# First layer's gate projection moved to its output stage, and a three-tile projection in the second input stage

## What is computed

```python
# layer 0, state-space part, 8 frames (images) to a sequence, 4 sequences
xz = einsum('bld,ed->ble', layer_norm(x_flat, ln1_w, ln1_b), in_proj_w)   # 96 -> 384
xm, z = split(xz, 2)                                                      # 192 and 192
y_f = ssm_branch(xm, z, ...)            # ... return y * silu(z)
y_b = ssm_branch(reversed xm and z, ...)[reversed]
x_m = x_flat + einsum('ble,de->bld', y_f + y_b, out_proj_w)               # then ln2
# layer 1
x = x + conv_ref(group_norm(x), W_in, b_in, ...)   # W_in: 96 -> 384, halves xx and z of 192
```

## Time and profile before

| what | value |
|---|---|
| median of 3 executions | 18361.85 us (18345.74 to 18377.84) |
| profiled execution, its own time | 18362.69 us |
| its span, first to last instruction | 18360.9 us |
| TensorE, VectorE, ScalarE, GpSimd busy in the whole span | 88%, 87%, 79%, 61% |
| mean granted TensorE clock | 0.962 of full |
| the input stage of layer 0 | from 0 to about 359 us |
| the output stage of layer 0 | from about 5499 to 5969 us |
| the input stage of layer 1 | from about 7216 to 7700 us |

### The profile page before, as it was taken

How to read it: one execution, slowest core, us unless ns; L and a number is a source line. 1 busy time by engine, 2 the same in 40 slices (tenths; PEclk the granted TensorE clock), 3 DMA queues, 4 the chain that set the end, 5 groups by cost and what they waited for, 6 DMA issues and landing times. The chain is left out here.

```text
span 18360.9 us, 268147 instructions
## 1 busy us (share of the span) xinstructions
PE 16077.0 (88%) x94216; PEld 11444.0 (62%) x94216; DVE 15910.4 (87%) x12063; ACT 14529.2 (79%) x23238; POOL 11254.5 (61%) x6343
## 2 busy tenths in 40 slices
PE   8799998899996788879888888888888888889798
PEld 3355554455552365455688888888888888647374
DVE  4799998799996486479899999999999999879698
ACT  7699996799992555557899999999999999745556
POOL 0099993499990475035688888888888888500201
PEclk9899999899997899989999999999999999999899
DMA  5788886788879677767777777777777777741323
GB/s 178 231 243 250 246 252 208 233 249 247 251 223 245 213 226 217 265 230 278 224 191 200 194 192 191 194 193 192 191 190 197 197 191 191 194 122 55 104 57 101
DMA packets 1043305, 3693.66 MB, mean 201 GB/s; under 512 B 162006, under 2 KB 196410, under 8 KB 1017404
## 3 DMA queue, kind: packets, MB, share of 16 engines
q1 hardware_dynamic: 815420, 3003.46, 53.8%
q0 software_dynamic: 147456, 536.94, 14.9%
q10 hardware_dynamic: 79104, 136.10, 2.4%
HBM read 2342.15 MB, written 796.94 MB: 171 GB/s over the span
## 5 line engine op out<-in xcount | busy, mean ns | idle before, releaser
L1832 DVE TENSOR_TENSOR_SCAN l1s_h<-l1s_da,l1s_pd 128x1024 f32<-128x1024 f32 x3072 | 6709.3, 2262 | 152.0 <-DMA l1s_h<-l1s_h 85.4
L1853 ACT ACTIVATE l1s_da<-l1s_dl,l1s_a 128x1024 f32<-128x1024 f32 x3072 | 3505.0, 1141 | 312.7 <-DVE l1s_h L1832 308.5
L1718 PE MATMUL l1s_pd<-l1s_bd,l1s_dut 128*128 128x128 f32 x18432 | 2847.5, 291 | 853.7 <-DVE l1s_h L1832 828.6
L1718 PEld LDWEIGHTS l1s_pd<-l1s_bd,l1s_dut 128*128 128x128 f32 x18432 | 2297.3, 191 | 1229.0 <-DVE l1s_h L1832 1092.0
L1870 ACT ACTIVATE l1s_dm<-l1s_dut,l1s_bt 128x384 f32<-128x384 f32 x5120 | 2888.2, 602 | 200.9 <-PE l1s_pd L1723 200.5
L1687 POOL TENSOR_TENSOR l1s_pb<-l1s_h,l1s_cc 128x1024 f32<-128x1024 f32 x1024 | 2423.4, 2367 | 843.7 <-DVE l1s_h L1832 802.6
L1687 POOL TENSOR_TENSOR l1s_pa<-l1s_h,l1s_cc 128x1024 f32<-128x1024 f32 x1024 | 2428.0, 2371 | 84.1 <-DMA l1s_h<-l1s_h 84.1
L1723 PE MATMUL l1s_pd<-l1s_id,l1s_dm 128*128 128x128 f32 x15360 | 2186.6, 273 | 0.1
L2702 POOL TENSOR_TENSOR l0sf_pr<-l0sf_h,l0sf_cc 128x1024 f32<-128x1024 f32 x768 | 1810.9, 2375 | 32.2 <-DVE l0sf_h L2784 27.0
L2702 POOL TENSOR_TENSOR l0sb_pr<-l0sb_h,l0sb_cc 128x1024 f32<-128x1024 f32 x768 | 1809.1, 2371 | 30.8 <-DVE l0sb_h L2784 26.8
L1723 PEld LDWEIGHTS l1s_pd<-l1s_id,l1s_dm 128*128 128x128 f32 x15360 | 1789.4, 142 | 0.6 <-ACT l1s_dm L1870 0.5
(11 more groups left out here) (323 smaller groups left out, 31362.7 us busy)
## 6 DMA issues: line engine op xcount, KB each, us to landing
l1s_cc<-crows SPq DMA_DIRECT2D x1024, 512.0 KB, 4.5
l1s_h<-l1s_h POOLq DMA_DIRECT2D x1024, 512.0 KB, 6.9
l0sf_cc<-l0crowsf SPq DMA_DIRECT2D x512, 512.0 KB, 6.3
l0sb_cc<-l0crowsb SPq DMA_DIRECT2D x512, 512.0 KB, 5.7
l0sf_cc<-l0crowsf SPq DMA_DIRECT2D x512, 256.0 KB, 8.5
l0sb_cc<-l0crowsb SPq DMA_DIRECT2D x512, 256.0 KB, 7.6
dls<-l1p_dl SPq DMA_DIRECT2D x192, 512.0 KB, 7.0
duts<-l1p_dut SPq DMA_DIRECT2D x64, 1536.0 KB, 6.6
```

The costliest lines, as they stand in the source:

```text
L1718: pe.matmul(pd[:, s % 2, blk * 128:blk * 128 + 128], dut[:, half, blk, j * 128:j * 128 + 128], bd[:, n, blk - SCALED, :], start=True, stop ...
L1832: dve.tensor_tensor_scan(tile(rnd, j), da[:, j, :], pd[:, s % 2, :], 0.0, ALU.mult, ALU.add)\
L1853: act.activation(da[:, j, :], dl[:, half, j, :], ACT.Exp, scale=a[:, HT * half + j, n:n + 1])\
```

## The change

The input stage of layer 0 no longer projects z. It projects the 192 outputs of xm as 128 + 64 rows, TensorE in the order var (k+1), mean (k+2), tiles of image k; ScalarE copies the first tile out, VectorE the second; the table of Ln and Exp is loaded once; and the normalised input is stored to DRAM (`xns`, 96 rows an image) in place of silu(z) (192 rows). The output stage loads those 96 rows as `zin`, projects z itself three images ahead (`widen`, as two tiles), and ScalarE applies Silu out of PSUM (`gate_of`), with tables loaded by name ahead of each. The output projection's PSUM tile is now single. The second layer's input stage has three tiles of 128 outputs; the middle one is emptied half by VectorE and half by ScalarE with Silu, the slot alternates by image, and the tables are loaded early, two to an image.

```diff
 def l0_in_proj(nc, x, w, xmp, xns):
-        out = r.sb("out", [C, 2, 4, HW])
+        out = r.sb("out", [128, 2, 2, HW])
@@ sync
-                        for q in range(4):
-                            sp.wait_ge(evac, nth(4 * k + q))
+                        sp.wait_ge(xnd, nth(k))
+                        sp.sem_inc(passed, 1)
+                        sp.dma_start(one(xns, FRAMES * s + c), xn[:, s, :]).then_inc(s_xn[s], 16)
+                        for q, (done, rows) in enumerate(((evac, slice(0, DLOW)), (evacd, slice(DLOW, DI)))):
+                            sp.wait_ge(done, nth(k))
                             sp.sem_inc(passed, 1)
-                            rows = slice((q % 2) * C, (q % 2 + 1) * C)
...
+                            sp.dma_start(xmp[s, rows, bass.ds(c * HW + PAD, HW)], out[0:rows.stop - rows.start, s % 2, q, :])\
+                              .then_inc(s_out[s % 2][q], 16)
@@ tensor
                 def project(k, s, q):
-                    pe.wait_ge(evac, nth(4 * k + q - 2))
+                    rows = DLOW if q == 0 else DHIGH
+                    pe.wait_ge(evac if q == 0 else evacd, nth(k - 1))
                     for hs in HALVES:
-                        mm = pe.matmul(pp[:, q % 2, hs], wt[:, q * C:(q + 1) * C], xn[:, s % 2, hs], start=True, stop=True)
+                        mm = pe.matmul(pp[0:rows, q, hs], wt[:, q * DLOW:q * DLOW + rows], xn[:, s, hs], start=True, stop=True)
                 def turn(c, s):
                     k = c * SEQS + s
-                    if there(k):
-                        pe.wait_ge(xnd, nth(k))
-                        for q in range(2):
-                            project(k, s, q)
                     c1, s1, k1 = ahead(c, s, 1)
                     if there(k1):
                         pe.wait_ge(sqr, nth(k1))
                         average(k1, s1 % 2, sq[:, s1 % 2, :]).then_inc(var, 1)
-                    if there(k):
-                        for q in range(2, 4):
-                            project(k, s, q)
                     c2, s2, k2 = ahead(c, s, 2)
                     if there(k2):
                         pe.wait_ge(s_in[s2], c2 * 16 + 16)
                         pe.wait_ge(lnv, nth(k2 - 2))
                         average(k2, s2 % 2, xin[:, s2, :]).then_inc(mean, 1)
+                    if there(k):
+                        pe.wait_ge(xnd, nth(k))
+                        project(k, s, 0)
+                        project(k, s, 1)
@@ vector: cent of k+2 first, then xn of k+1, then
+                    if there(k):
+                        dve.wait_ge(proj, nth(2 * k + 1))
+                        dve.wait_ge(s_out[s % 2][1], (k - s % 2) * 8)
+                        dve.tensor_copy(out[0:DHIGH, s % 2, 1, :], pp[0:DHIGH, 1, :]).then_inc(evacd, 1)
@@ scalar: the table's load moved ahead of the turns; Ln, Exp, Square, then
+                    if there(k):
+                        act.wait_ge(proj, nth(2 * k))
+                        act.wait_ge(s_out[s % 2][0], (k - s % 2) * 8)
+                        act.activation(out[:, s % 2, 0, :], pp[:, 0, :], ACT.Copy).then_inc(evac, 1)

 def l0_out_proj(nc, x, ysf, ysb, xns, w, xm, n2):
-        po = r.ps("po", [C, 2, HW]); pm = r.ps("pm", [C, 2, HW])
+        po = r.ps("po", [C, HW]); pm = r.ps("pm", [C, 2, HW]); pz = r.ps("pz", [128, HW])
@@ sync, load
+                    sp.dma_start(zin[:, s, :], one(xns, FRAMES * s + c)).then_inc(s_zin[s], 16)
...
-                    sp.dma_start(z[:, s, 0, :], one(zs[:, 0:DLOW, :], image)).then_inc(s_in[s], 16)
-                    sp.dma_start(z[0:DHIGH, s, 1, :], one(zs[:, DLOW:DI, :], image)).then_inc(s_in[s], 16)
                     sp.dma_start(xin[:, s, :], one(x, image)).then_inc(s_in[s], 16)
@@ tensor
+                def widen(k, s, q):
+                    rows = DLOW if q == 0 else DHIGH
+                    pe.wait_ge(silu, nth(2 * k + q - 1))
+                    for hs in HALVES:
+                        mm = pe.matmul(pz[0:rows, hs], wz[:, q * DLOW:q * DLOW + rows], zin[:, s, hs], start=True, stop=True)
+                    mm.then_inc(wide, 1)
...
+                    if there(k3):
+                        pe.wait_ge(s_zin[s3], c3 * 16 + 16)
+                        widen(k3, s3, 0)
                     if there(k):
                         pe.wait_ge(sqr, nth(k))
                         average(s % 2, sq).then_inc(var, 1)
...
                         average(s1 % 2, xo).then_inc(mean, 1)
+                    if there(k3):
+                        widen(k3, s3, 1)
                     if there(k2):
                         pe.wait_ge(gate, nth(2 * k2 + 1))
-                        pe.wait_ge(resid, nth(k2 - 2))
+                        pe.wait_ge(resid, nth(k2 - 1))
@@ scalar
-                act.preload_act_table_set("natural_log_exp_and_others")
+                def gate_of(k, s, q):
+                    rows = slice(0, DLOW if q == 0 else DHIGH)
+                    act.wait_ge(wide, nth(2 * k + q))
+                    act.wait_ge(proj, nth(k - SEQS))
+                    act.activation(z[rows, s, q, :], pz[rows, :], ACT.Silu).then_inc(silu, 1)
...
+                    if there(k3):
+                        act.preload_act_table(ACT.Silu)
+                        gate_of(k3, s3, 0)
+                    act.preload_act_table_set("natural_log_exp_and_others")
                     if there(k):
... Ln and Exp of image k
+                    if there(k3):
+                        act.preload_act_table(ACT.Silu)
+                        gate_of(k3, s3, 1)
                     if there(k1):
... Square of image k+1

 def l1_in_proj
-        out = r.sb("out", [128, 4, HW])
+        out = r.sb("out", [128, 3, HW])
@@ vector
-                        for q in (0, 1):
-                            dve.wait_ge(proj, nth(4 * k + q))
+                        for q, rows in ((0, slice(0, 128)), (1, slice(0, DHIGH))):
+                            dve.wait_ge(proj, nth(3 * k + q))
                             dve.wait_ge(s_out[q], k * 16)
-                            dve.tensor_scalar(out[:, q, :], pp[:, q % 2, :], bi[:, q:q + 1], None, ALU.add).then_inc(evacd, 1)
+                            dve.tensor_scalar(out[rows, q, :], pp[rows, (s + q) % 2, :], bi[rows, q:q + 1], None, ALU.add)\
+                               .then_inc(evacd, 1)
@@ tensor
-                        pe.wait_ge(evac, nth(2 * (k - 1) + q % 2))
-                        if q >= 2:
-                            pe.wait_ge(evacd, nth(2 * k + q % 2))
+                        if q < 2:
+                            pe.wait_ge(evac, nth(2 * (k - 1) + q))
+                        if q == 0:
+                            pe.wait_ge(evacd, nth(2 * (k - 1) + 1))
+                        if q == 2:
+                            pe.wait_ge(evacd, nth(2 * k))
                         for hs in HALVES:
-                            mm = pe.matmul(pp[0:m, q % 2, hs], wi[:, at:at + m], xc[:, p, hs], start=True, stop=True)
+                            mm = pe.matmul(pp[:, (s + q) % 2, hs], wi[:, q * 128:q * 128 + 128], xc[:, p, hs], start=True, stop=True)
...
                     if there(k):
                         project(2)
-                        project(3)
@@ scalar
+                        act.preload_act_table_set("natural_log_exp_and_others")
... Ln and Exp of image k+1
+                    if there(k):
+                        act.preload_act_table(ACT.Silu)
+                        gated(k, s, 1, slice(DHIGH, 128))
... Copy of image k+2, which gives `summed`
                     if there(k):
-                        for q in (2, 3):
...
+                        gated(k, s, 2, slice(0, 128))
```

More of the change, by code:

```diff
@@ L128, in stream, with l0_in_proj @@
         sp.wait_ge(s_x[s], 16 * IMAGES // 2)
-def l0_in_proj(nc, x, w, xmp, zs):
+def l0_in_proj(nc, x, w, xmp, xns):
     with ExitStack() as stack:
@@ L181, in _ @@
                 for p in range(2):
-                    for q in range(4):
+                    for q in range(2):
                         sp.wait_ge(s_out[p][q], 16 * IMAGES // 2)
+                for s in range(SEQS):
+                    sp.wait_ge(s_xn[s], 16 * FRAMES)
             @block.tensor
@@ L227, in turn @@
                 def turn(c, s):
[L228 to L236, removed]
+                    k = c * SEQS + s
                     c2, s2, k2 = ahead(c, s, 2)
@@ L243, in turn @@
                         dve.tensor_tensor(xc[:, p, :], xin[:, s2, :], pm[:, p, :], ALU.subtract).then_inc(cent, 1)
+                    c1, s1, k1 = ahead(c, s, 1)
+                    if there(k1):
+                        p = s1 % 2
+                        dve.wait_ge(rstd, nth(k1))
+                        dve.wait_ge(proj, nth(2 * (k1 - SEQS) + 1))
+                        dve.wait_ge(s_xn[s1], c1 * 16)
+                        dve.scalar_tensor_tensor(out=xn[:, s1, :], in0=xc[:, p, :], scalar=lnw[:, 0:1],
```

(34 more changed lines are left out.)

62 lines of the change are left out of this document (23 added, 39 removed).

## The result

The changed kernel takes 18120.22 us (median of 4, 18111.13 to 18126.40) against 18356.37 us for the kernel before (median of 4). The ratio is 0.9871, 95% interval 0.9859 to 0.9883, so 236 us less. In a second session on another chip it was 18132.97 against 18361.51, ratio 0.9880 (0.9863 to 0.9896). Forecast were 18142 us and a range of 18095 to 18235.

A forecast was written before the change was run, and what follows sets the result against it. TensorE was taken to bind both input stages (with a ScalarE handshake in the second layer's) and transfers the output stage. Gains 108 + 39 + 73 = 220 us from 18362 gave 18142 us, range 18095 to 18235.

The forecast's parts named there:

- First input stage: Layer 0's input stage: TensorE binds, 24 passes become 16, 10.32 to 6.95 us an image, gain 108 us.
- Rival E: Early-loaded tables and reordering do nothing, only passes count; second layer's input period 13.0, total gain 192, 18170 us; chance 0.05.
- Output stage: Layer 0's output stage: transfers bind, 864 rows become 768, 13.53 to 12.2 us an image, gain 39 us.
- reads only: Layer 0's output stage: if only rows read count, 576 of 672, the period is 11.60 us an image.
- The clock surcharge: Layer 0's output stage: 0.2 us an image added in case some TensorE passes run at the low clock.
- Rival A: Output stage loses through TensorE's clock staying at 0.79: period 14.5, stage loses 30 us, total 18211 us; chance 0.09.
- rival D: Slower than before: TensorE at 1.2 GHz throughout the output stage, 20.7 us an image, 18403 us; decides from 20.0; chance 0.02.
- Rival C: ScalarE bounds the output stage, table loads costing 2.6 us instead of 1.28: 13.1 us an image, 18168 us; chance 0.02.
- level with the transfer bound, not above it: Output stage: TensorE's new wait for zin would cost only 0 to 0.7 us, being level with the transfers' limit.
- Second layer's input stage: Layer 1's input stage: TensorE loses 4 passes and a 1.24 us wait, 14.40 to 12.1 us an image, gain 73 us.
- 0.3 of hand-over: Second layer's input stage before the change: 0.3 us of hand-over counted within its 14.05 us an image.
- Rival B: Transfers bind both input stages, loads landing late: periods 7.5 and 12.9 us, gain 175, total 18187 us; chance 0.12.

The follow-up runs named there:

- The tiles of 96: Changed kernel with the first input stage's 192 outputs as 96 + 96 instead of 128 + 64: 18113.72 us, ratio to before 0.9867.
- the early load: Changed kernel with the load of zin issued one turn earlier in the output stage: 11.64 us an image, whole kernel 18132.65 us.
- the run without x: Changed kernel loading x for the first four images only in layer 0's output stage, without layer 1's early table loads: 10.64 us an image there, 18085.51 us in all.

## Why the prediction was right

The total was 22 us above the measured median and the range held it. The three terms were each close too (108, 39 and 73 us forecast, 98, 60 and 80 measured), but part of that closeness is luck: the first was too high where the second was too low, and the second is not known to better than some 15 us. The terms one by one:

- **First input stage, right in mechanism, 0.28 us an image short.** "What is left is 16 passes, 6.89 us" counted passes only. The term that was missed is the change of width, 0.3 us an image for going into the 64-wide tile and out of it. The tiles of 96 gave 6.92, 0.03 under the forecast. ScalarE, VectorE and the landing of x stayed off the path, as said (x lands in 4.5 us in the changed kernel). The order had no term of its own: the prediction said that the loops close in time, but not what another order would lose. With TensorE's tiles first, it is 9.8 us an image. Rival E falls in its part on the reordering as far as TensorE's order goes; in its part on the early table loads it holds, since without them the second layer's stage kept its 11.95 us.
- **Output stage, right in what binds, too small in size.** The bound was put at 768/864 of 13.53, 12.03, and 0.2 added for the clock. Measured are 11.65; against the 13.15 that the same code of before also showed, 768/864 gives 11.69. The base was one execution of a stage that varies by 3%. The prediction's other count, reads only, gave 11.60 from the base of 13.53, and no run parts these two readings. The clock surcharge was not due: the granted clock was 0.99 with a pause of about 1 us a turn. Rival A falls with it, and rival D, whose limit is mis-summed: 181 us lost by this stage are 31 x 5.84, so it would decide from 19.4 us an image and not 20.0. Rival C falls by the rows of the table load. The step on the wait for zin, "level with the transfer bound, not above it", is shown by the early load.
- **Second layer's input stage, right.** 11.75 us in an undisturbed turn against 11.8, and the new wait for `summed` is there, 0.83 for the 1.0 forecast. The "0.3 of hand-over" in the count for the stage before was not identified there; it fits the 64-wide fourth tile, which went with the change. The mean is 11.93 and not 12.1, since the clock was 0.99 and not 0.96. The wait of 1.24 us before tile 0 was counted at its own length; with fixed slots a wait of 0.90 there costs 2.5 us an image, because the clock falls with it. That part of its worth was missing in the argument, and rival E's 13.0 for this stage was too low for the same reason.
- **Rival B**: the shares were 0.67 and 0.96 (0.72 and 0.93 forecast) and TensorE hardly waited for a load (1.7 us in 4 waits in the second layer's stage), so it falls. VectorE does wait for stores there (112.7 us in 29 waits between 7090 and 7430), off the path.

## What to carry to other kernels

When TensorE binds a stage, count its passes, and then look at what stands between them. A wait can cost more than its length, because the granted clock may fall with it: here 0.90 us cost 2.5. Removing work from the engine that binds may open such a pause and lose more than the work was worth, unless the engines' orders fit what is left: with TensorE's tiles first, 16 passes took 17.0 us an image where 24 had taken 10.3. And when the wait list names one load, move that load earlier. If the wait only moves to another load and the time stays, as with zin, then not this load's place but the transfers as a whole may set the stage; move fewer bytes to find out, as in the run without x.

## What the runs showed of the hardware that was not expected

- Eight more passes a turn made a stage faster: 24 passes at a granted clock of 1.00 took 10.8 us an image, 16 at 0.60 took 17.0.
- Two waits of TensorE, 0.83 and 0.90 us in a turn of 12.8 to 16.1, went with a mean granted clock of 0.87; the first of them alone, in a turn of 11.75 us, with 0.99.
- A weight of 64 columns between wider ones costs 0.14 us going in and 0.17 going out, with 0.43 us between passes otherwise; from 96 to 128 columns (158.86 to 159.29) and back (5621.56 to 5621.99, both in the changed kernel's trace) the loads follow at 0.43.
- A stage that the DMA engines set differed by 15 us of 470 between executions of the same code, while the changed input stage of layer 0, which TensorE sets, took 257.0 to 258.1 us in eight traces of the same code.
